# Gather indices of a graph network kept in SBUF and copied pass by pass by VectorE

## The reference

```python
h = relu(layernorm(x)); x = x + L0(h)      # four layers of GENConv, below
h = relu(layernorm(x)); x = x + segment_sum(h[dst] * edge_weight, src)

def _genconv(x, src, dst, ea, W1, b1, lg, lb, W2, b2, t):
    m = relu(x[src] + ea) + EPS            # ea = edge_attr @ eencW + eencb
    logits = m * t
    mx = segment_max(logits, dst)
    e = exp(logits - mx[dst])
    alpha = e / segment_sum(e, dst)[dst]
    h = segment_sum(m * alpha, dst) + x
    return relu(_ln(h @ W1 + b1, lg, lb)) @ W2 + b2
```

## Time and profile before

| | us |
|---|---|
| median of 3 runs | 12002.17 (11963.65 to 12016.73) |
| the profiled execution, time | 11994.87 |
| the profiled execution, span from first to last instruction | 11993.1 |
| first gather of layer 0, of layer 1 | 143.96, 2603.27 |
| first indirect DMA of the third stage | 9924.88 |

### The profile page before, as it was taken

The page is one execution under the profiler, slowest core; times in us unless marked ns, Lnnn a source line. Parts: engine busy times, 40 slices in busy tenths (PEclk is TensorE's granted clock), DMA queues, the critical chain, the costliest instruction groups (busy, mean ns, idle before and its releaser), DMA issues. The chain is left out here.

```text
span 11993.1 us, 107333 instructions
## 1 busy us (share of the span) xinstructions
PE 5746.9 (48%) x30526; PEld 4148.6 (35%) x30526; DVE 5926.9 (49%) x7860; ACT 3290.7 (27%) x4928; POOL 6801.0 (57%) x6468
## 2 busy tenths in 40 slices
PE   2333434344433433433433434334433447888887
PEld 2333323233333322333333333233332334555554
DVE  4443434344444433443444434344443447888887
ACT  1332323233333322332333333223332332111110
POOL 5555555544555555455555554555555546888887
PEclk8666666666666666666666667666666668999998
DMA  4332323222223223222232322223222324555554
GB/s 121 95 88 80 93 82 93 80 66 86 88 87 96 86 81 88 71 84 82 88 88 88 93 86 75 74 86 94 87 88 82 90 84 97 96 92 98 94 94 84
DMA packets 849217, 1051.23 MB, mean 88 GB/s; under 512 B 559309, under 2 KB 598787, under 8 KB 847351
## 3 DMA queue, kind: packets, MB, share of 16 engines
q1 hardware_dynamic: 522594, 822.25, 20.8%
q0 software_dynamic: 322624, 224.55, 12.8%
q10 hardware_dynamic: 3916, 3.40, 0.1%
HBM read 612.22 MB, written 437.38 MB: 88 GB/s over the span
## 5 line engine op out<-in xcount | busy, mean ns | idle before, releaser
L675 POOL DMA_INDIRECT xg<-h_tab,idx x4992 | 4775.5, 957 | 4283.3 <-issue 2983.0
L709 PE MATMUL turn<-ident,ea 128*64 128x128 f32 x10368 | 1112.0, 398 | 3280.8 <-issue 1700.6
L907 DVE TENSOR_TENSOR_SCAN rx<-rp,carry,zl 128x1536 f32<-128x1536 bf16 (+1 forms) x224 | 740.7, 3307 | 3572.0 <-ACT zl L820 2843.5
L709 PEld LDWEIGHTS turn<-ident,ea 128*64 128x64 f32 x10368 | 975.1, 211 | 3417.0 <-issue 1744.8
L1201 POOL DMA_INDIRECT acc<-vm,tgt x1026 | 1597.0, 1557 | 381.8 <-issue 298.9
L828 ACT ACTIVATE st_all<-turn 128x512 f32<-128x512 f32 (+1 forms) x1344 | 751.3, 578 | 2316.5 <-remote 1789.0
L810 ACT ACTIVATE at<-turn 128x512 f32<-128x512 f32 (+1 forms) x672 | 374.8, 579 | 3178.8 <-remote 2430.6
L718 PEld LDWEIGHTS zl<-ident,xg 128*128 128x128 f32 x5184 | 849.2, 226 | 817.6 <-issue 740.2
L733 PE MATMUL turn<-ident,num 128*128 128x128 f32 x2592 | 630.5, 399 | 973.4 <-issue 737.5
L718 PE MATMUL zl<-ident,xg 128*128 128x128 f32 x5184 | 863.9, 310 | 381.1 <-issue 322.2
L715 PE MATMUL zl<-at,attrW 128*128 128x512 f32 (+1 forms) x1344 | 900.0, 755 | 230.1 <-issue 162.5
(11 more groups left out here) (254 smaller groups left out, 6962.4 us busy)
## 6 DMA issues: line engine op xcount, KB each, us to landing
sums<-st_all SPq DMA_DIRECT2D x416, 768.0 KB
ea<-in_edge_attr_dram SPq DMA_DIRECT2D x420, 384.0 KB
srcB<-src_flat SPq DMA_DIRECT2D x108, 768.0 KB
rp<-run_pen SPq DMA_DIRECT2D x420, 192.1 KB
xg<-h_tab,idx POOLq DMA_INDIRECT x4992
run_head<-zeros SPq DMA_DIRECT2D x216, 192.0 KB
hd<-run_head SPq DMA_DIRECT2D x108, 384.0 KB
run<-run_pen SPq DMA_DIRECT2D x108, 192.0 KB
```

The lines of the kernel that those rows point to most:

```text
L675: g_.indirect_dma_start(xg[b][:, k, h, :], None, h_tab[:, :], bass.IndirectOffsetOnAxis(ap=idx[b][:, h, k:k + 1] if small is None else idx ...
L709: ins = pe.matmul(ps[6 + (b + gr) % 2][h * D:(h + 1) * D, j * P:(j + 1) * P], ea[b][:, h, gr * gt + j, :], ident[:, :], start=True, stop=True)
L907: link(v.tensor_tensor_scan(rx[:, 0:width], rp[b][:, 0:width], zl[:, 0:width], carry[:, 0:1], ALU.min, ALU.max))
```

## The change

All gather indices of the full passes are loaded into SBUF once, before the first layer, into `idx_full` (54 places: 52 passes and the first two once more). The two small buffers `idx` stay, and POOL's gathers read them as before; but DVE fills them, with one copy of 128 x 24 int32 for each full pass (`next_lists`), placed ahead of its first scan of the pass two before, behind the same wait for `l_ok`. POOL waits for that copy (`idx_ok`). SP's two `idx` loads of every pass go. To make room in SBUF, `src_t` lies in the space of `xin`, and therefore the load of x now waits for the five list stores, and the memset of `xin` stands behind them.

```diff
+            idx_full = sb("idx_full", [P, FULLW + 2, 2, K], I32, c)
-            src_t = sb("src_t", [ROWS, W], F32, c)
+            src_t = xin.rearrange("p t d -> p (t d)")[0:ROWS, 0:W]
...
-                            sp.dma_start(idx[b][:, h, :], src[piece].rearrange("(p k) -> p k", k=K)).then_inc(idx_in[b], 16)
...
+                    def load_lists(place, w0, w1):
+                        for h in range(2):
+                            begin = h * HALF + w0 * W
+                            sp.dma_start(idx_full[:, place:place + w1 - w0, h, :], src[begin:begin + (w1 - w0) * W]
+                                         .rearrange("(w p k) -> p w k", p=P, k=K)).then_inc(idx_full_in, 16)
...
+                    load_lists(0, 0, 2)
                     load(0, 0, 0)
                     load(1, 1, 1)
-                    sp.wait_ge(pads_ok, 4)
+                    sp.wait_ge(pads_ok, 3)
+                    load_lists(2, 2, FULLW)
+                    load_lists(FULLW, 0, 2)
                     load_small_lists()
...
+                    sp.wait_ge(out_lists, 16 * 5)
+                    sp.wait_ge(pads_ok, 4)
                     sp.dma_start(xin[0:N // NT, :, :].rearrange("p t d -> p (t d)"),
...
-                            g_.wait_ge(idx_in[b], 32 * (l * FULL_PAIRS + i + 1))
+                            g_.wait_ge(idx_ok, l * FULLW + w + 1)
...
+                    lists = idx_full.rearrange("p w h k -> p (w h k)")
+                    v.wait_ge(idx_full_in, 32)
+                    for b in range(2):
+                        v.tensor_copy(idx[b].rearrange("p h k -> p (h k)"), lists[:, b * 2 * K:(b + 1) * 2 * K]).then_inc(idx_ok, 1)
...
+                    def next_lists(w, b):
+                        v.tensor_copy(idx[b].rearrange("p h k -> p (h k)"), lists[:, bass.ds(w * 2 * K, 2 * K)]).then_inc(idx_ok, 1)
...
                         v.wait_ge(l_ok, g + 1 + L0)
+                        if width == W:
+                            next_lists(w + 2, b)
...
-                    v.memset(xin[96:P, :, :], 0.0).then_inc(pads_ok, 1)
...
+                    v.wait_ge(out_lists, 16 * 5)
+                    v.memset(xin[96:P, :, :], 0.0).then_inc(pads_ok, 1)
                     v.wait_ge(fx_in, 16)
...
+                    v.wait_ge(idx_full_in, 16 * 6)
                     with v.Fori(0, L) as l:
```

More of the change, by code:

```diff
@@ L458, in gnn @@
             idx = [sb(f"idx{i}", [P, 2, K], I32, c) for i in range(2)]
+            idx_full = sb("idx_full", [P, FULLW + 2, 2, K], I32, c)
+            idx_ok, idx_full_in = sem("idx_ok"), sem("idx_full_in")
             idx_last = sb("idx_last", [P, LAST, 2, K // 2], I32, c)
@@ L510, in gnn @@
             xg_in = [[sem(f"xg_in{i}_{gr}") for gr in range(NG)] for i in range(2)]
-            ea_in, idx_in, rp_in, st_out = (
-                [sem(f"{n}{i}") for i in range(2)] for n in ("ea_in", "idx_in", "rp_in", "st_out"))
+            ea_in, rp_in, st_out = (
+                [sem(f"{n}{i}") for i in range(2)] for n in ("ea_in", "rp_in", "st_out"))
             z_ps, u_ok, l_ok, diff_ok, ex_ok, max_ok, sums_ok, back_ps, back_sb = (
@@ L658, in _ @@
                     for b in range(2):
-                        sp.wait_ge(idx_in[b], 32 * (FULL_PAIRS * L + 1))
                         sp.wait_ge(ea_in[b], 32 * (PAIRS * L + 1))
@@ L664, in _, with window @@
                 def _(g_):
-                    def window(g, i, l, b, gt=GT, small=None):
+                    def window(g, w, l, b, gt=GT, small=None):
                         if small is None:
-                            g_.wait_ge(idx_in[b], 32 * (l * FULL_PAIRS + i + 1))
+                            g_.wait_ge(idx_ok, l * FULLW + w + 1)
                             g_.sem_inc(gather_go, 1)
@@ L684, in _ @@
                             for b in range(2):
-                                window(l * LW + 2 * i + b, i, l, b)
+                                window(l * LW + 2 * i + b, 2 * i + b, l, b)
                         for s in range(LAST):
-                            window(l * LW + FULLW + s, FULL_PAIRS + s // 2, l, s % 2, GT // 2, s)
+                            window(l * LW + FULLW + s, None, l, s % 2, GT // 2, s)
                         for b in range(2):
@@ L790, in _ @@
                 def _(a):
-                    a.wait_ge(pads_ok, 4)
+                    a.wait_ge(pads_ok, 3)
                     whole_rows = ROWS_REAL * W
```

## The result

The changed kernel takes 12308.1 us (four runs, 12297.3 to 12310.8) against 11982.9 us for the kernel before (four runs): ratio 1.027, 95% interval [1.024, 1.030]. It is slower, as forecast, by 325 us and not by 640. Run again later, the same kernel gave 1.031 [1.022, 1.040].

What follows compares the result with a forecast made beforehand. Bound: the chain to zl, held up while POOL gathers. A pass: 0.4 restart + 29.9 gathers + 15.0 tail + 0.2 copy = 45.5 against 42.3 us, times 196, plus 15 for the start: 12640 us; 8-in-10 range 11400 to 13260.

Runs made afterwards that it cites:

- spaced_224: Changed kernel plus a 128x224 int32 iota on GpSimd, awaited, behind each gather of the full passes, gathers 1.46 us apart; 10529.4 us, ratio 0.876 to before.
- copy_late: Changed kernel with VectorE's list copy moved behind the two scans of the maximum; 9150.3 us where nothing stands (ratio 1.0013), 12459.0 us where engines stand (1.040).

## What to carry to other kernels

Where one engine's stream slows the others, take the pace from when the stream starts and how much of it there is, and sort the places of the old trace by just that before a median is taken: a median over two states fits neither. A wait that an engine has "for nothing" can be what lets the others work; removing it only moves it, as here, where a release 2.9 us earlier decided between 2.7% slower and 2.4% faster. And look at the stream itself first: a filler of 0.2 us behind each gather was worth more than all of the change.

## What was unexpected of the hardware

- The slowing of PE, ACT and SP beside a stream of gathers depends on the distance of the gathers: full at 1.26 us, and between 1.44 and 1.46 it all but ends. It lasts 33.9 to 34.1 us for 24 gathers that take 28.9, 30.0 or 32.7 us, and 67.8 for 48. Halving the rows of each gather leaves it as it is.
- It depends on the chip: the same kernel before took 9137 us on one and some 12000 on every other that was seen. The kernels profiled there have the same gathers, 1.26 us apart. Why that chip differs is open. What spacing costs on such a chip was not run; 24 x 1.46 = 35.0 us of gathers against 30.2 would make it a loss there.
- What the place is stays open. ACT and PE stand with nothing to wait for, and in rows 7's double burst PE gets its matmuls one by one 0.70 us apart, half of 1.41. The DMA engines are not full: in the changed kernel the stretch from 3565 to 3575 shows a DMA share of 0.14. And from 3576.5 to 3579.3, the last 2.8 us before ACT is back, no engine and no DMA does anything at all. So it is not the moving of the gathered rows that the others wait for; that had ended.

```profile
3565.00:3570.00 5.00, 0.74 (x2) 0.58 (x2) 0.00 (x0) 0.00 (x0) 3.78 (x5) 0.50 0.14 26
3570.00:3575.00 5.00, 0.74 (x2) 0.58 (x2) 0.00 (x0) 0.00 (x0) 3.78 (x5) 0.50 0.14 26
```

```profile
3576.50:3579.30 2.80, 0.00 (x0) 0.00 (x0) 0.00 (x0) 0.00 (x0) 0.00 (x0) 0.50 0.00 0
```

  (Columns: the window and its length, busy time of PE, PE's weight load, DVE, ACT and POOL, granted clock, DMA share, GB/s.) PE from the kernel before:

```profile
3093.05 0.37 PE L718 MATMUL zl<-ident,xg 128*128 128x128 f32 x1 [0.33 <-issue]
3093.76 0.37 PE L718 MATMUL zl<-ident,xg 128*128 128x128 f32 x1 [0.33 <-issue]
3094.46 0.37 PE L718 MATMUL zl<-ident,xg 128*128 128x128 f32 x1 [0.33 <-issue]
```

- The Trainium skill (Runtime: NRT & Kernel Launch, "Instruction fetch mechanics") says that each sequencer fetches its next instructions through a DMA queue of its own, mostly hidden. A delayed fetch would look like these stands, but the profile speaks against it. It has packets of the kind "instruction", 83 in the whole run of the changed kernel (packets, MB, share of 16 engines):

```profile
q8 instruction: 44, 0.72, 0.0%
q14 instruction: 39, 0.32, 0.0%
```

  and from 2800 to 4970 us, where some 49 passes have their stands, the queues are these two alone:

```profile
q1 hardware_dynamic: 42505, 142.25, 18.4%
q0 software_dynamic: 37738, 38.72, 9.5%
```

- DVE does not stand. In the middle of ACT's stand it begins the scan for `num` at 3559.97, 0.03 us after its instruction before, and the scan takes the 3.41 us that it also takes on the chip where nothing stands.
- The copy of DVE takes 474 ns on average in `spaced_224`, against 185 in the changed kernel, where POOL is silent. In 130 of the 208 copies it begins within a gather and ends with it, as here:

```profile
4012.04 0.96 POOL L689 DMA_INDIRECT xg<-h_tab,idx  x1 [0.17 <-POOL pause L695]
4012.31 0.68 DVE L928 COPY idx<-idx_full 128x24 int32 x1 [15.21 <-ACT zl L839]
```

  So here the gather seems to hold the copy, and not the copy the gather. It doesn't always: in `copy_late` the copies begin within a gather too and take 0.15 us. What makes the difference was not tried.
